# A three-layer sequence block on one core: v fetched through DRAM instead of spread by the PE array, and state units re-cut

## What is computed

```
state[k, d, 0]  = state taken from ctx
state[k, d, t]  = decay[k, t-1] * state[k, d, t-1] + key[k, t-1] * v[d, t-1]
att[d, t]       = sum_k r[k, t] * state[k, d, t]  +  v[d, t] * sum_k u[k] * r[k, t] * key[k, t]
```

## Time and profile before

| | before |
|---|---|
| median of 3 runs | 2303.19 us |
| the profiled execution | 2301.0 us |
| its span, first to last instruction | 2299.2 us |
| PE busy | 2141.9 us (93%) |
| DVE busy | 1952.8 us (85%) |
| ACT busy | 1260.4 us (55%) |
| POOL busy | 585.2 us (25%) |
| mean DMA rate | 30 GB/s |

### The profile page before, as it was taken

The page is one execution under the profiler, slowest core; times in us unless marked ns, Lnnn a source line. Parts: engine busy times, 40 slices in busy tenths (PEclk is TensorE's granted clock), DMA queues, the critical chain, the costliest instruction groups (busy, mean ns, idle before and its releaser), DMA issues. The chain is left out here.

```text
span 2299.2 us, 41734 instructions
## 1 busy us (share of the span) xinstructions
PE 2141.9 (93%) x14176; PEld 1477.2 (64%) x14176; DVE 1952.8 (85%) x4863; ACT 1260.4 (55%) x4405; POOL 585.2 (25%) x700
## 2 busy tenths in 40 slices
PE   3698799999999999999999999999999999999866
PEld 2475576767666676767667676766767676666533
DVE  0258898989899898989989898999989899998982
ACT  1736374573838466383746648373755738374312
POOL 1131314222331422232141322224141222314200
PEclk7799899999999999999999999999999999999977
DMA  7100101001010100001010100101010010100000
GB/s 268 35 7 20 31 11 49 11 11 41 11 50 11 49 11 31 21 11 50 11 49 11 48 3 11 50 11 50 11 49 1 11 50 11 50 2 29 1 19 10
DMA packets 48978, 69.88 MB, mean 30 GB/s; under 512 B 20512, under 2 KB 26656, under 8 KB 48768
## 3 DMA queue, kind: packets, MB, share of 16 engines
q1 hardware_dynamic: 48768, 67.21, 8.9%
HBM read 50.42 MB, written 16.78 MB: 29 GB/s over the span
## 5 line engine op out<-in xcount | busy, mean ns | idle before, releaser
L1226 DVE TENSOR_TENSOR_SCAN st<-ws,st 128x256 f32<-128x256 f32 x1024 | 637.4, 686 | 0.1
L862 ACT ACTIVATE probs_or_mixes<-probs_or_mixes,least 128x128 f32<-128x128 f32 x1024 | 398.9, 403 | 117.4 <-DVE least L1173 116.3
L1215 DVE TENSOR_TENSOR st<-bank_pair,kT 128x1016 f32<-128x1016 f32 x256 | 308.0, 1203 | 88.0 <-PE bank_pair L717 88.0
L1236 DVE TENSOR_TENSOR st<-st,rT 128x1024 f32<-128x1024 f32 x256 | 317.9, 1243 | 0.0
L1173 DVE CUSTOM_DVE_ANT_0 probs_or_mixes<-bank,nmask 128x128 f32<-128x128 f32 x1024 | 231.1, 285 | 100.5 <-PE bank L566 76.0
L1108 POOL TENSOR_SCALAR rstd<-rstd 128x1 f32<-128x1 f32 x96 | 26.5, 276 | 1098.4 <-ACT cin L895 600.1
L1102 POOL TENSOR_TENSOR probs_or_mixes<-probs_or_mixes 128x512 f32<-128x512 f32 x160 | 190.1, 1218 | 341.4 <-DVE probs_or_mixes L1267 341.4
L862 ACT ACTIVATION_READ_ACCUMULATOR probs_or_mixes<-probs_or_mixes,least 128x1 f32 x1024 | 206.4, 202 | 0.0
L717 PE MATMUL bank_pair<-v_hi,sel 32*128 32x256 f32 x1024 | 193.8, 339 | 10.9 <-DVE st L1215 10.6
L717 PE MATMUL bank_pair<-v_lo,sel 32*128 32x256 f32 x1024 | 166.6, 286 | 0.0
L717 PEld LDWEIGHTS bank_pair<-v_hi,sel 32*128 32x128 f32 x1024 | 114.5, 185 | 72.3 <-issue 35.4
(11 more groups left out here) (150 smaller groups left out, 4216.3 us busy)
## 6 DMA issues: line engine op xcount, KB each, us to landing
inputs_turned<-in_ctx_turned SPq DMA_DIRECT2D x16, 512.0 KB, 3.6
inputs_turned<-in_x_turned SPq DMA_DIRECT2D x16, 512.0 KB, 4.6
xin<-in_x SPq DMA_DIRECT2D x16, 512.0 KB, 3.7
x<-xin SPq DMA_DIRECT2D x16, 512.0 KB, 4.1
keep<-x SPq DMA_DIRECT2D x16, 512.0 KB, 3.6
out<-keep SPq DMA_DIRECT2D x32, 256.0 KB, 2.0
wo<-in_wo SPq DMA_DIRECT2D x2, 1024.0 KB, 11.3
nmask<-in_mask SPq DMA_DIRECT2D x16, 128.0 KB, 4.1
```

Source lines behind the costliest of these rows:

```text
L862: last = fn(pr[:, n % 4, j, :], pr[:, n % 4, j, :], ACT.Exp, bias=least[:, n, j:j + 1], scale=-1.0, accum_out=rsum[:, n, j:j + 1])
L1215: tt(dst, src, over(kv, DU, 1), ALU.mult).then_inc(outer.sem, 1)
L1226: last = nc.vector.tensor_tensor_scan(v, ws[:, c].rearrange("p b t -> p (b t)"), v, 0.0, ALU.mult, ALU.add)
L1236: tt(v, v, over(rT[:, u // PER, :], DU, 1), ALU.mult).then_inc(weighed.sem, 1)
```

## The change

1. v is no longer spread by PE. ACT's `proj_v` writes one fp32 tile `vT`; the sync queue stores it to a DRAM tensor `v_rows` (two transfers of 64 partitions per half of the chunks, `save_v`), and fetches it again per unit straight into a slot of `st`, each of 8 rows of 4 KB repeated to 16 partitions (`spread`, now a step of SP). `v_hi`, `v_lo`, the DVE and POOL work on them, `bank_pair` and the fp32r `sel` go.
2. A unit is two value columns of two chunks, again 1024 columns; a scan covers 512. `reduce` adds with 512-column matmuls over four steps into all of bank 7. `bonus`, `readout` and `rk` work per pair of chunks; the bonus has a bank of the ring, readout frees bank 7 by a semaphore of its own.
3. Five slots instead of four, each 4 columns longer; the fetch lands one column later than the value's own, so `outer` multiplies in place. `outer` and `first` wait for the landing (`v_there`).
4. The ring has six banks.
5. All four lists are ordered anew, and SP gets one.

```diff
-UNIT_D = [(0, 1, 8, 9), (4, 5, 12, 13), (2, 3, 10, 11), (6, 7, 14, 15)]
+HALF_T = 2 * T
+UNIT_D = [(4 * (w % 2) + w // 2, 8 + 4 * (w % 2) + w // 2) for w in range(2 * PER)]
-SLOTS = 4
+SLOTS = 5
+PITCH = DU * T + 4
...
 PE_ORDER = """
+low.0+1 key.0 low_rank.0+1 reduce.5+2 low_rank.2+1 tdecay.0+1 value.0 proj_r.0+1 decay.0+1 proj_v.0+1 proj_k.0+1
+decay.1+1 reduce.6+2 reduce.7+2 query.0 var.0+2 proj_r.1+1 score.0 score.2 rstd.0+2 query.1 proj_g.0+1 proj_g.1+1
+turn_p.0 score.4 turn_p.1 turn_p.2 turn_p.3 score.6 out.0+2 out.1+2 turn_p.4 score.8 turn_p.5 values.0 reduce.0+1
+turn_p.6 turn_p.7 score.10 proj_v.1+1 turn_p.8 flip.0 score.12 reduce.1+1 values.1 turn_m.0+2 turn_p.9 turn_p.10
+proj_k.1+1 score.14 share.0 turn_p.11 turn_p.12 turn_m.1+2 reduce.2+1 values.2 project.0 turn_p.13 turn_p.14
+turn_p.15 flip.1 reduce.3+1 share.1 values.3 project.1 ffn_k.0+2 ffn_r.0+2 ffn_k.1+2 ffn_r.1+2 reduce.4+1 turn_n.0
+turn_n.1 ffn_v.0+2 ffn_v.1+2
...
 ACT_ORDER = """
+low.0+1 first.13+2 key.0 tdecay.0+1 first.14+2 state.1+1 first.15+2 proj_r.0+1 square.0+2 keep_row.0+1 proj_v.0+1
+decay.0+1 proj_k.0+1 decay.1+1 state.2+1 first.0+1 square.1+2 query.0 proj_r.1+1 score.0 score.1 first.1+1 first.2+1
...
 POOL_ORDER = """
+mix.0+1 mix.1+1 mix.2+1 mix.3+1 rk.0+1 negate.0 mix.4+1 bias.0 bias.1 norm2.0+2 norm2.1+2 norm0.0 affine0.0 norm0.1
+affine0.1 rk.1+1 norm1.0 norm1.1
...
 DVE_ORDER = """
+weigh.11+2 mix.0+1 mix.1+1 mix.2+1 weigh.12+2 mix.3+1 outer.13+2 outer.14+2 scan.13+2 scan.14+2 value.0 outer.15+2
+weigh.13+2 weigh.14+2 scan.15+2 weigh.15+2 mix.4+1 readout.1+2 outer.0+1 outer.1+1 var.0+2 score.0 score.1 score.2
+scan.0+1 groupnorm.0+2 scan.1+1 score.3 proj_g.0+1 outer.2+1 weigh.0+1 proj_g.1+1 score.4 score.5 outer.3+1 scan.2+1
+score.6 score.7 out.0+2 scan.3+1 weigh.1+1 out.1+2 score.8 outer.4+1 weigh.2+1 score.9 inverse.0 weigh.3+1 score.10
+score.11 scan.4+1 outer.5+1 score.12 weigh.4+1 scan.5+1 outer.6+1 score.13 weigh.5+1 scan.6+1 weigh.6+1 gather.0
+score.14 outer.7+1 score.15 scan.7+1 project.0 inverse.1 weigh.7+1 shift2.0+2 gather.1 outer.8+1 scan.8+1 project.1
+outer.9+1 outer.10+1 scan.9+1 readout.0+1 outer.11+1 weigh.8+1 weigh.9+1 outer.12+1 scan.10+1 scan.11+1 shift.0
+weigh.10+1 scan.12+1 ffn_v.0+2 ffn_v.1+2
...
+SP_ORDER = """
+load_c.0 spread.5+2 spread.6+2 save_v.1+2 spread.7+2 spread.8+2 spread.9+2 spread.10+2 load_m.0 load_s.0+1 load_s.1+1
+spread.11+2 spread.12+2 save.0+1 spread.13+2 load_x.0 spread.14+2 load_t.0 store.0+3 bring.0+2 spread.15+2 load_s.2+1
+load_s.3+1 save_v.0+1 spread.0+1 spread.1+1 spread.2+1 spread.3+1 spread.4+1
...
-RING, READOUT = [0, 1, 2, 4], 7
+RING = [0, 1, 2, 4, 5, 6]
...
+        def slot(g, u):
+            return (UNITS * g + u) % SLOTS
+        def v_there(eng, g, u):
+            eng.wait_ge(landed[slot(g, u)], ((UNITS * g + u) // SLOTS + 1) * 16)
...
+            def save_v(g, p):
+                wait(sp, outer.sem, outer.after(g - 1, 2 * PER * (p + 1)))
+                key = ("proj_v", p)
+                sp.wait_ge(emptied[XB.of(key)], XB.through(key, g))
+                for half in range(2):
+                    sp.dma_start(v_rows[p, :, half], vT[64 * half:64 * half + 64, 2 * p:2 * p + 2, :]
+                                 .rearrange("p c n -> p (c n)")).then_inc(v_saved[p].sem, 16)
+            def spread(g, u):
+                p = u // (2 * PER)
+                sp.wait_ge(v_saved[p].sem, v_saved[p].after(g, 2))
+                wait(sp, summed.sem, summed.after(g, (u - SLOTS) // 2 + 1))
+                r = HC * UNIT_D[u % (2 * PER)][0]
+                src = v_rows[p, r:r + HC].rearrange("h s n -> h (s n)")
+                n = slot(g, u)
+                sp.dma_start(st[:, n, 1:DU * T + 1],
+                             src.unsqueeze(1).to_broadcast([HC, HD, DU * T])).then_inc(landed[n], 16)
...
             def reduce(g, q):
-                m, c = q % 2, q // 2
+                p, m = q // PER, q % PER
                 if m == 0:
-                    bonus(g, c)
+                    wait(pe, read_out.sem, read_out.after(g, p))
+                if m == PER - 1:
+                    bonus(g, p)
                 pe.wait_ge(weighed.sem, weighed.after(g, 2 * q + 2))
+                o = 24 - 8 * m
+                for s in range(2):
                     for u in (2 * q, 2 * q + 1):
+                        r = 64 * s + 32 * (u % 2)
+                        last = mm(bank[7][r:r + 32, :], ebase[:, o:o + 32],
+                                  st[:, slot(g, u), s * HALF_T:(s + 1) * HALF_T], start=m == 0, stop=m == PER - 1)
...
             def outer_(g, u):
+                v_there(dve, g, u)
+                dst = st[:, slot(g, u), 0:DU * T].rearrange("p (s r t) -> p s r t", s=2, t=L)[:, :, :, 1:]
+                kv = kT[:, 2 * p:2 * p + 2, :].rearrange("p c (b t) -> p (c b) t", b=NB)[:, :, 0:L - 1]
+                tt(dst, dst, over(kv, 2, 1), ALU.mult).then_inc(outer.sem, 1)
...
             def scan(g, u):
+                for s in range(2):
+                    v = st[:, slot(g, u), s * HALF_T:(s + 1) * HALF_T]
+                    last = nc.vector.tensor_tensor_scan(v, ws[:, 2 * p:2 * p + 2].rearrange("p c b t -> p (c b t)"), v, 0.0,
+                                                        ALU.mult, ALU.add)
```

More of the change, by code:

```diff
@@ L121 @@
 PE_ORDER = """
[L122 to L126, removed]
@@ L134 @@
[L134 to L138, removed]
@@ L152 @@
[L152 to L156, removed]
@@ L493, in _ @@
             for it in range(G + LATEST):
-                turn(it)
+                for name, n, late in SP_STEPS:
+                    g = it - late
+                    if known(g) and not (g == 0 and name in FIRST):
+                        does[name](g, n)
             sp.wait_ge(stored.sem, stored.after(G, 0))
@@ L699, in proj @@
                 return step
-            def spread(g, u):
-                c = u // PER
-                if first_group(g) and u == 0:
-                    pe.wait_ge(loaded_w[3], W_COUNT[3])
-                    pe.wait_ge(sel_ready, 1)
-                if u % (2 * PER) == 0:
-                    key = ("proj_v", u // (2 * PER))
-                    pe.wait_ge(emptied[XB.of(key)], XB.through(key, g))
-                wait(pe, outer.sem, outer.after(g, u))
-                for k in range(2):
-                    for part in (v_hi, v_lo):
-                        for s in range(2):
-                            d = UNIT_D[u % PER][2 * s + k]
-                            r = slice(32 * (d // 4), 32 * (d // 4) + 32)
-                            last = mm(pair[:, s, k * T:(k + 1) * T], sel[r, d % 4, :], part[r, c, :],
-                                      start=part is v_hi, stop=part is v_lo)
-                last.then_inc(spreaded.sem, 1)
@@ L721, in bonus @@
-            def bonus(g, c):
-                pe.wait_ge(rk_done.sem, rk_done.after(g, c + 1))
-                ps, full = y_bank(("readout", c), g)
-                mm(ps[:, T:2 * T], ublk[:, c, :], rk[:, c % 2, :], start=True, stop=True).then_inc(full, 1)
+            def bonus(g, p):
+                pe.wait_ge(rk_done.sem, rk_done.after(g, p + 1))
+                ps, full = y_bank(("bonus", p), g)
+                for q in range(2):
+                    last = mm(ps[:, q * T:(q + 1) * T], ublk[:, 2 * p + q, :], rk[:, q, :], start=True, stop=True)
+                last.then_inc(full, 1)
@@ L1000, in square @@
             def square(g, p):
-                hold(act, emptied, g, through("readout", 2 * p + 1))
+                act.wait_ge(read_out.sem, read_out.after(g, p + 1))
                 hold(act, filled, g, through("ffn_r", NB - 1, back=1))
```

222 lines of the change are left out of this document (83 added, 139 removed).

## The result

The changed kernel takes **2372.5 us** (median, 2369.43 to 2376.24), the one before 2302.64 beside it: ratio 1.0304, 95% interval 1.0286 to 1.0322. It is 70 us slower where 115 us less were forecast.

The account below looks back on a forecast made before the run. PE's queue was taken as the bound, DVE second. A period of 123.3 us plus 0.8 slot waiting and 1.4 for chance meetings gave 125.5; 16 x 125.5 + 176 + 4 = 2188 us, range 2130 to 2262.

Parts of the forecast that it names:

- DVE's contention term: In outer on DVE: reading both inputs from SBUF beside POOL costs 27 ns x 16 = 0.4 us a period.
- backlog of PE: DVE's 88.0 us in 33 waits for bank_pair come from PE's full queue, not from missing data.
- DVE's other terms: On DVE a period: longer scans save 1.7 us, the dropped v_lo subtraction 1.2, readout 0.5.
- PE's demand: On PE: removing 16 spreads saves 10.2 us a period, taking its work from 130.8 to 120.6 us.
- chance meetings: PE at 97% and DVE at 96% load must sometimes wait on each other: 1.4 us added a period.
- The seam: From PE's ffn_v through var to the period's end: sum 123.3 us, plus 0.8 us waiting for outer.1's slot.
- first rival: Fetches from 8 source rows use half the engines: 2 to 3 us more a period, 2228 us; chance 0.25.
- The forecast's latency: In the slot loop: a fetch of 512 KB lands in 4.6 us, the save of v in 2.5.
- the sign of an error: Signs of a wrong forecast: DVE's fetch waits over 3 us a period, or DVE idle above 8 us with banks and slots free.
- the rest of the period was 87.3: The period after var: 87.3 us before; less nine spreads (5.9), plus reduce.4 (1.0), gives 82.4.
- The rival that ended slower: v's way through DRAM delays outer.0: at 5 us more per transfer the period is 135.5, 2348 us; chance 0.07.
- Filling and draining: Start and end outside the 16 periods: 176 us, bounds 168 and 184, against 178 before.

Follow-up runs that it names:

- e1: The kernel before, with outer's first input read from an SBUF tile instead of bank_pair, spreads and waits kept: 2353.73 us.
- e12: The changed kernel with affine0 on DVE, rk.1 behind the norm, two copies of v in DRAM, and POOL's ten mix additions cut to one column: 2197.0 us.
- e5: The changed kernel with rk.1 moved behind norm1.0 and norm1.1 in POOL's order: 2351.06 us.
- e6: The changed kernel with affine0's four instructions moved from POOL to DVE and rk.1 last on POOL: 2272.88 us.
- e10: The kernel before with affine0 moved from POOL to DVE: 2300.12 us, ratio 0.9988.
- e7: The kernel before without the spread matmuls on PE and the waits on them: 2272.84 us.
- e4: The changed kernel with five banks in the ring and outer's first input read from zeros in a PSUM bank: 2423.24 us.
- e3: The changed kernel with five banks in the ring instead of six: 2490.54 us.
- e8: The changed kernel with v stored twice in DRAM, so a fetch reads 16 rows repeated to 8 partitions: 2346.85 us.
- e2: The changed kernel with only the first five units fetched, stores kept, later waits on the slot's sums instead of landings: 2351.08 us.

## Why the prediction was wrong

**The step that failed is DVE's contention term**: "27 ns x 16 = 0.4 us a period" for an outer product with both inputs in SBUF. It was priced by `weigh`, whose mean lay 27 ns above its median. But in the old order `weigh` seldom met POOL at work, to judge by its short tail. The scans did meet it, which the prediction didn't read:

```profile
L1226 DVE TENSOR_TENSOR_SCAN st<-ws,st x1024: 654/665/1751, 150.7 to 2232.9; 128x256 f32<-128x256 f32 x171
```

Their longest took 1.1 us over the median, as much as the long ones of the new kernel. In the new order `outer` and `weigh` meet POOL too: the outer product's mean rose by 275 ns, 16 x 0.275 = 4.4 us a period, and `weigh`'s by 130 ns, 2.1 us. I quoted the rule that explains it, that of the Trainium skill (SBUF — State Buffer, "SBUF: two separate sides"), under which such an instruction and one of GpSimd that reads SBUF wait for each other. The timelines, e1 and e12 agree with it. I priced it as a mean over few meetings, where each meeting costs up to the whole length of the other engine's instruction (2.29 us for 1.21), and the number of meetings is what the change raised.

**The same term had another side, which I left out entirely**: POOL's instructions grow too. I had read that ACT and POOL "have room" and costed nothing there. But POOL's norm chain between `project.1` and `turn_n` is in series with PE. Its end went from 5.4 to 12.7 us, 2.3 of that by `rk.1`, a step that POOL's new order moved into the chain and that I never costed. PE waited 7.1 us a period behind them, and PE's clock fell in that gap. e5 (21 us), e6 (100 us) and the control e10 (3 us) show the hold-up of POOL as the largest loss, though e6 also takes meetings away from DVE.

The operand in SBUF is only one cause of the longer chain. In the old order with that operand it takes 5.9 us (e1); without DVE's pause and with the operand in PSUM 7.1 (e7); in the new order with the operand in PSUM 11.1 (e4). The prediction booked DVE's 88.0 us of waiting for `bank_pair` as backlog of PE that would turn into gain. 4.9 us of it a period were the time in which POOL's chain ran undisturbed.

**DVE's other terms were right.** Two scans of 512 that meet no POOL instruction take 2.25 us to the start of what follows (1077.19 to 1079.44 in the changed kernel), where 2.23 was forecast. Scans: 637.4 us in 16 periods before; e12, with fewer meetings, has 609.9, which is 1.7 less a period as forecast; in the changed kernel only 0.7 of it is left. With -1.2 for `v_lo` and -0.5 for the readout as forecast, DVE's sum is 121.6 - 0.7 - 1.2 - 0.5 + 4.4 + 2.1 = 125.7 us a period, measured 126.5; I had 118.6.

**PE's demand was near, its worth was not.** Forecast 120.6 us; e12, at clock 1.00, has 120.89, and the changed kernel 123.63 at 0.96. e7, at clock 1.00 in the old order, has 123.11, so there the spreads gave 7.7 us and not 10.2. And e7 shows that the relief alone moves the old kernel by 29 us, since the two engines' waits on each other grow in its place. The 1.4 us that I added for "chance meetings" was too little for that order. In the new one the sixth bank alone is worth 118 us (e3).

**The seam and the transfers.** The forecast found 0.8 us of waiting at outer.1, and had a fetch on half the engines as its first rival at 2 to 3 us a period and a chance of 0.25. e8 confirmed the cause; the price was 26 us in all, 1.6 a period. The forecast's latency was too short as well: with all engines a fetch lands in 5.5 us in the median (e8) and not in 4.6, and five of them in a row, at 122 GB/s, keep the changed kernel's engines at work for 21 us. DVE's waits on fetches add up to 47.1 us in 22 waits, 2.9 a period, just under the 3 named as the sign of an error; DVE's idle time, 10.3 us of a period, was over the 8 named. The seam that mattered was the other end of the period, at `turn_n`, where I had carried over the old spacing whole ("the rest of the period was 87.3").

**The rival that ended slower named the wrong mechanism.** It put a price of 2348 us on v's way through DRAM; e2, without the fetches, is at 2351.08. That the two numbers lie close is chance.

Filling and draining: ten periods from the mark at 556.92 to that at 1935.70 give 137.9 us, and 2373.0 - 16 x 137.9 = 167 us against 176 forecast, just under its lower bound of 168. Nothing hangs on it.

The forecast's 125.5 us a period and 2188 us in all are near e12, in which POOL's mixes are out of the way: 125.35 in its late period, 126.3 in the mean of eleven (marks at 520.33 and 1909.37 us), and 2197.0 us. In part that is luck, since e12 has `affine0` on DVE, two copies of v, and a DVE that is busy 122.39 us and not 118.6.

What stays open: how the 100 us of e6 divide, how much of the longer chain each cause has in the changed kernel itself, and why the ring of five costs 118 us.

## What to carry to other kernels

Moving an operand of a large VectorE instruction from PSUM to SBUF has to be paid twice: in VectorE's own time wherever GpSimd works beside it, and in every GpSimd instruction of a chain that another engine waits for, short ones above all. The same holds for removing a wait of VectorE: its pause may be the time in which GpSimd works undisturbed. An engine at 33% of a period may still hold the critical chain, so read for each of its short chains who waits at the end and whether VectorE is idle beside it, and price its instructions as if they ran in turns with the full engine. If such an operand must move, clear the chain first (here four instructions moved to VectorE and `rk.1` behind the norm turned 3% slower into 1% faster), and repeat the source rows of a broadcast fetch until there are 16.
